# A macaron block with a selective scan: another planned order of its instructions, and the scan carries copied later

## The reference

```
x = x + 0.5 * ffn(layernorm(x))       # silu(g) * u with 1408 hidden units, ternary weights
x = x + ssm(layernorm(x))
x = x + 0.5 * ffn(layernorm(x))       # the same weights

ssm: h, gate = x @ W_in (1024 channels each)
     h = silu(causal_conv4(h))
     ts, B, C = h @ Wx, each rms-normed (128, 16 and 16 values)
     delta = softplus(ts @ Wdt + bias)
     for each channel i and n in 0..15, over time t:
         s[t] = exp(delta[t] * A[i,n]) * s[t-1] + delta[t] * B[t,n] * h[t]
     y[t] = sum over n of s[t] * C[t,n] + D * h[t];  out = (y * silu(gate)) @ Wout
```

## Time and profile before

| | us |
|---|---|
| median of three executions | 2842.37 |
| lowest, highest | 2838.3, 2843.48 |
| profiled execution, its own time | 2835.58 |
| its span, first to last instruction | 2833.8 |
| VectorE busy in the span | 2466.0 |
| TensorE busy | 2386.6 |
| GpSimd busy | 2275.5 |
| ScalarE busy | 1757.4 |
| mean granted clock of TensorE, of 1 | 0.922 |

### The profile page before, as it was taken

The page is one execution under the profiler, slowest core; times in us unless marked ns, Lnnn a source line. Parts: engine busy times, 40 slices in busy tenths (PEclk is TensorE's granted clock), DMA queues, the critical chain, the costliest instruction groups (busy, mean ns, idle before and its releaser), DMA issues. The chain is left out here.

```text
span 2833.8 us, 38163 instructions
## 1 busy us (share of the span) xinstructions
PE 2386.6 (84%) x12266; PEld 1933.5 (68%) x12266; DVE 2466.0 (87%) x3115; ACT 1757.4 (62%) x2995; POOL 2275.5 (80%) x1387
## 2 busy tenths in 40 slices
PE   6779789689577998889988999889988886599968
PEld 5657677577466776677766877677776764477756
DVE  5649997897998989899999999899989988999973
ACT  5465667767656666576657765577657666465531
POOL 2257769779976889789996999779996889889852
PEclk9889899899789999999999999999999997599979
DMA  8655645846666467955778366955778388366544
GB/s 268 225 191 167 238 160 178 297 131 230 205 214 235 127 211 265 310 172 172 248 267 314 129 216 237 322 202 166 235 266 283 121 287 289 101 206 188 183 165 141
DMA packets 293952, 606.66 MB, mean 214 GB/s; under 512 B 23024, under 2 KB 23792, under 8 KB 293744
## 3 DMA queue, kind: packets, MB, share of 16 engines
q1 hardware_dynamic: 293744, 604.13, 63.5%
HBM read 451.47 MB, written 152.57 MB: 213 GB/s over the span
## 5 line engine op out<-in xcount | busy, mean ns | idle before, releaser
L1930 POOL TENSOR_TENSOR sbuf<-dus,bring 128x1024 f32<-128x1024 f32 x512 | 1217.9, 2394 | 181.3 <-PE pt L1403 94.4
L1556 ACT ACTIVATE pa<-dls,cst 128x512 f32<-128x512 f32 x1024 | 691.8, 688 | 432.3 <-DVE sbuf L1730 415.8
L1403 PE MATMUL pt<-ident,sbuf 128*128 128x128 f32 x4096 | 645.0, 294 | 210.9 <-DVE sbuf L1730 84.1
L1403 PEld LDWEIGHTS pt<-ident,sbuf 128*128 128x128 f32 x4096 | 507.2, 150 | 367.4 <-DVE sbuf L1730 131.9
L1322 PE MATMUL pm<-xT,wring 128*128 128x512 f32 x2816 | 708.0, 399 | 16.1 <-DVE xT L1613 6.4
L1730 DVE TENSOR_TENSOR_SCAN sbuf<-pa,sbuf 128x512 f32<-128x512 f32 x512 | 610.0, 1211 | 64.6 <-ACT pa L1556 53.4
L1730 DVE TENSOR_TENSOR_SCAN sbuf<-pa,carry,sbuf 128x512 f32<-128x512 f32 x512 | 631.9, 1268 | 35.2 <-POOL sbuf L1930 23.1
L1334 PE MATMUL pm<-wring,act 128*128 128x512 f32 x2176 | 581.4, 410 | 25.1 <-DVE hd L1658 9.4
L1322 PEld LDWEIGHTS pm<-xT,wring 128*128 128x128 f32 x2816 | 516.6, 189 | 120.3 <-issue 18.4
L1741 DVE SCALAR_TENSOR_TENSOR acc<-pt,cT,acc 128x512 f32<-128x512 f32 x768 | 548.0, 739 | 51.6 <-PE pt L1403 49.9
L1334 PEld LDWEIGHTS pm<-wring,act 128*128 128x128 f32 x2176 | 401.6, 193 | 113.4 <-issue 14.4
(11 more groups left out here) (142 smaller groups left out, 2285.9 us busy)
## 6 DMA issues: line engine op xcount, KB each, us to landing
wring<-wsp SPq DMA_DIRECT2D x408, 512.0 KB, 4.5
bring<-b_d SPq DMA_DIRECT2D x256, 256.0 KB, 3.9
xn_d<-tb SPq DMA_DIRECT2D x24, 1024.0 KB, 9.1
xnb<-xn_d SPq DMA_DIRECT2D x19, 1024.0 KB, 7.3
x_d<-tb SPq DMA_DIRECT2D x16, 1024.0 KB, 6.1
u_d<-hd SPq DMA_DIRECT2D x64, 256.0 KB, 5.7
sg_d<-hd SPq DMA_DIRECT2D x64, 256.0 KB, 4.3
tb<-x_d SPq DMA_DIRECT2D x16, 1024.0 KB, 6.8
```

What stands on the lines that cost most here:

```text
L1403: ins = e.matmul(pt[u.pt[tt]][:, k * P:(k + 1) * P], sbuf[:, u.s3, k, tt * P:(tt + 1) * P], ident[:, :], is_transpose=True, start=True, st ...
L1556: e.activation(pa[k % 2][:, :], dls[:, k, :], ACT.Exp, scale=col(C_A + (4 * u.ig + k) * N + u.n)).then_inc(S.a_exp, 1)
L1930: e.tensor_tensor(sbuf[:, u.s3, h * m:(h + 1) * m, :], dus[:, h * m:(h + 1) * m, :], bring[:, u.s2:u.s2 + 1, :].broadcast_to([P, m, TC]), ...
```

## The change

The planner's costs change: MARGIN goes from 0.3 to 0.12, LATE of TensorE from 0.3 to 0.2 (the others by 0.01 or 0.02), VectorE's fixed cost from 0.05 to 0.064. TensorE's matmuls have no fixed cost any more: each is a number of columns (at least 256), and the new class Columns counts columns in stretches of 3.4133 us of the plan's time. A matmul runs at 2270 columns a microsecond in the plan where the stretch before has counted 3060 or more, else at 1200. These are constants of the plan. The emitted instructions are the same ones; their order on each engine is what the new plan gives.

The carry copy moves within ScalarE's thread s: the Book hands each step the even step before it (behind), and the copy for that one is issued after the second exponential (k == 1) of the next step. The copy of an even chunk's last step is issued in the first step of the odd chunk. A scan of an odd chunk now waits for the copy of its own ig and n, where it waited for the last copy made.

```diff
--- before.py
+++ after.py
@@ -71,10 +71,12 @@
     "sp": {},
 }
 SPARE = {("pe", "t"): 0.4, ("act", "t"): 0.0, ("pool", "t"): 0.0, ("act", "s"): 0.0, ("pool", "s"): 0.0}
-MARGIN = 0.3
+MARGIN = 0.12
 DWELL = 12.0
+
+WINDOW, BUSY, FULL, HALF_RATE = 3.4133, 3060, 2270.0, 1200.0
 ISSUE, LAND = 0.42, 2.5
-LATE = {"pe": 0.3, "act": 0.13, "dve": 0.13, "pool": 0.15}
+LATE = {"pe": 0.2, "act": 0.12, "dve": 0.14, "pool": 0.17}
 PEF = 1.12
 
 
@@ -117,6 +119,7 @@
 
     def begin(self):
         self.events, self.time, self.up, self.table = [], 0.0, None, None
+        self.columns = ()
 
     def wait_ge(self, *events):
         self.events += events
@@ -128,14 +131,14 @@
         if self.eng == "act":
             self.time += 0.09 + n / 1190.0 + more
         elif self.eng == "dve":
-            self.time += 0.05 + n / 962.0 + more
+            self.time += 0.064 + n / 962.0 + more
         else:
             self.time += 0.16 + n / 474.0 + more
         return self
 
     def matmul(self, out, a, b, is_transpose=False, **k):
         n = width(out)
-        self.time += 0.115 if is_transpose else 0.16 if n < 256 else n / 2140.0
+        self.columns += (max(256, n), 2 * n if is_transpose else n),
         return self
 
     def activation(self, out, a, f, bias=None, scale=None, **k):
@@ -181,12 +184,32 @@
         return self
 
 
+class Columns:
+
+
+    def __init__(self):
+        self.count = {}
+
+    def run(self, t, work):
+        for n, counted in work:
+            left = 1.0
+            while left > 1e-9:
+                k = int(t / WINDOW + 1e-9)
+                whole = n / (FULL if self.count.get(k - 1, 0.0) >= BUSY else HALF_RATE)
+                part = min(left, ((k + 1) * WINDOW - t) / whole)
+                self.count[k] = self.count.get(k, 0.0) + part * counted
+                left -= part
+                t += part * whole
+        return t
+
+
 class Plan:
 
 
 
     def __init__(self):
         self.reach, self.now, self.clock, self.owner = {}, {}, {}, {}
+        self.columns = Columns()
         self.table, self.switched, self.dma = None, 0.0, 0.0
 
     def order(self, threads):
@@ -232,7 +255,7 @@
                         at += 1.3
                         self.switched = at
                     self.table = s.table
-                end = at + s.time
+                end = self.columns.run(at, s.columns) if eng == "pe" else at + s.time
                 self.clock[eng] = end
                 end += LATE[eng]
             if s.up is not None:
@@ -282,6 +305,7 @@
         self.check = None
         self.stores = []
         self.scans, self.turns, self.softs = 0, 0, 0
+        self.carried, self.behind = {}, None
         self.first_stage()
 
     def up(self, sem, by=1):
@@ -969,7 +993,8 @@
                         load_u(1, 2 * h + 1)
             self.sfree["b", u.s2] = (u.prod[-1],)
             u.pa_before, u.exp, u.scan = [], [], []
-            u.carry_in = sf("carry") if second else ()
+            u.carry_in = self.carried[u.ig, u.n] if second else ()
+            u.behind = self.behind
             for k in range(4):
                 u.pa_before.append(sf(("pa", k % 2)))
                 u.exp.append(self.up(S.a_exp))
@@ -981,11 +1006,11 @@
                 self.sfree["pa", k % 2] = (u.scan[k],)
             if second:
                 self.sfree["carry_rd"] = (u.scan[3],)
-                u.carry = ()
+                u.carry, self.behind = (), None
             else:
                 u.carry_before = sf("carry_rd")
-                u.carry = (self.up(S.a_carry),)
-                self.sfree["carry"] = u.carry
+                u.carry = self.carried[u.ig, u.n] = (self.up(S.a_carry),)
+                self.behind = u
             self.add("t", u)
             u.ct = self.x_small[c].ct
             u.pt, u.pt_before, u.tr, u.acc_before, u.mul, u.sum = [], [], [], [], [], []
@@ -1556,11 +1581,12 @@
                         e.activation(pa[k % 2][:, :], dls[:, k, :], ACT.Exp,
                                      scale=col(C_A + (4 * u.ig + k) * N + u.n)).then_inc(S.a_exp, 1)
                         yield
-                    if not u.second:
-                        q.wait_ge(u.scan[3], *u.carry_before)
-                        e.activation(carry[:, u.n, 4 * u.ig:4 * u.ig + 4], sbuf[:, u.s3, :, TC - 1],
-                                     ACT.Copy).then_inc(S.a_carry, 1)
-                        yield
+                        if k == 1 and u.behind:
+                            v = u.behind
+                            q.wait_ge(v.scan[3], *v.carry_before)
+                            e.activation(carry[:, v.n, 4 * v.ig:4 * v.ig + 4], sbuf[:, v.s3, :, TC - 1],
+                                         ACT.Copy).then_inc(S.a_carry, 1)
+                            yield
             return program
 
         def act_states(units):
```

## The result

The changed kernel takes 2807.23 us (median of four runs, 2800.55 to 2812.57) against 2840.34 of the kernel before (four runs): a ratio of 0.9877, 95% interval 0.985 to 0.9905. The forecast was 2809. Its profiled execution took 2812.57 us around a span of 2810.7. That is the slowest of its four, and the profiled one of before (2835.58) was faster than all four of its own, so the two traces lie 23.1 us apart and not 33. The remaining 10 us are in no trace.

A forecast was written before the change was run, and what follows sets the result against it. The prediction took VectorE's work in a written order, plus its holes, to bound the middle. Carry -25, rates -4 and room -4 us sum to -33, taking the median 2842.4 to 2809 us; range 2775 to 2850.

The forecast's parts named there:

- The bound: Middle of the kernel: VectorE's work in a written order plus its holes, 209.5 us the most any order gives back.
- -25 for the carry: Even chunks' scans: moving the carry copy frees the next exponential, making their holes like odd chunks'; 25 us gained.
- a filled hole may only reach the next one: Even chunks' scans: reason for taking the carry's gain as 25 us, a little less than the row's 29.4.
- -4 for the rates: Middle at granted clock 0.5: planning TensorE's two rates cuts VectorE's idle time; 4 us gained, 21.2 at stake.
- -4 for the room: Hand-overs between engines: less planned room and VectorE's new fixed cost place consumers nearer to where they can run; 4 us.
- The sum: Whole kernel: carry, rates and room give -33 us, opening and tail nothing; median 2809 us.
- Its own sign of being wrong: Middle: wrong if VectorE's holes don't fall by 25 us or more; another sign was opening or tail changing by over 5.
- Slack gone: Rival at hand-overs: with 0.3 us less cover, just-in-time ones come late and holds pass on; 2872 us, chance 0.15.
- The product takes its place: Rival at the scans: they wait for GpSimd's product instead of the exponential, most gain returns; 2838 us, chance 0.18.
- The order hardly changes: Rival in the planner: same heads win, only the carry counts; 2817 us, inside the forecast's band, no separate chance.

The follow-up runs named there:

- found2: Changed kernel with other planner values (MARGIN 0.048, other LATE, SPARE and VectorE fixed cost), picked for the finished order's end in one cost table; 2786.3 us.
- carry_only: Against the kernel before: carry copy moved and the order planned anew with all the old costs; 2879.8 us, ratio 1.0131.
- margin13: Changed kernel with MARGIN 0.13 in place of 0.12 and nothing else; 2845.4 us, ratio 1.0004.
- the frozen order: Kernel before with its order kept on every engine and only the carry copies moved in ScalarE's queue; 2838.9 us, ratio 0.9983.
- costs_only: Changed kernel with the carry copy put back in its old place, all planner costs new; 2872.6 us, ratio 1.0102.

## Why the prediction was right, and where it was not

**The bound.** Right. In all fourteen kernels VectorE's busy time stays within 2457 to 2468 us, while their spans go from 2790 to 2876. All but those 11 us is its holes: 332 us in found2, 349 in the changed kernel, 368 in before, 418 in carry_only.

**Step "-25 for the carry".** Wrong as a worth of the move. The mechanism is as described: nearly all of the 0.85 us holes go, the copy never waits, and the changed kernel's product doesn't wait for it (in margin13 it does once, for 11.9 us, where the prediction put the later release at nothing). But its worth was 4.6 us in the old order, a loss of 36 planned anew with the old costs, a gain of 65 with the new ones and nothing with MARGIN 0.13. The error was to read the difference between even and odd chunks (29.4 us) as time that the end would see. A hole ahead of a scan, with queues written around it, is room that other waits fill: in the frozen order's trace 16.3 us went and 14.7 came back at the transposes. "a filled hole may only reach the next one" stood in the prediction, as a discount of 4 us; in the frozen order it was some 20 of the 25.

**Steps "-4 for the rates, -4 for the room".** Too small as parts, and no parts: from carry_only the rates give 33, the room 9, both 73. Each of these numbers is one order. The prediction took 4 for the room "since no row says which holes a new order closes"; that was the step that mattered, and no row could price it.

**The sum.** -33 forecast and -33 measured. With MARGIN 0.13 the same working would have forecast the same number and missed by 36 us. It is a right number by terms of which none is shown, and that is luck. Its own sign of being wrong, holes of the middle that fall by less than 25 us, came true (19.8).

**The rivals.** "Slack gone" is not borne out as a mechanism: found2 has a smaller MARGIN (0.048) and a smaller room at TensorE's t than the change and is faster (its ScalarE's t has 0.1 more), and margin13 has more room and is slower. "The product takes its place" is what happened in carry_only, with a price of 36 us above before and not 4 under. "The order hardly changes" was the worst reading: the order is what changes. The rival that was missing: that the planner's choice, stirred by a constant that means next to nothing, moves the time by more than any term of the sum. MARGIN's hundredth cost 38 us with the copy moved and gave 31 with it in its old place (2872.6 to 2841.5). Not every stir does that: the shifted stretches cost 8.

**What stays open.** Whether the move helps on average over many sets of costs. Of three pairs planned at equal costs one gains (2872.6 to 2807.2), one doesn't (2841.5 and 2845.4) and one loses (2843.6, the kernel before on that chip, to 2879.8). For the rates and the room nothing is known beyond their one order each. The new order with the copy put back wasn't tried. And what makes the changed kernel's order a good one isn't shown, only that it is the order.

## What to carry to other kernels

When an order comes out of a greedy planner, a measured hole is no price for the change that removes it: freeze the order to price the edit (a low price, since that order was planned without it), and move an unrelated constant by a hundredth to see how far orders scatter, before reading any gain as the edit's. Then choose the order by its own end under one fixed table of costs taken from a trace, over many sets of planning constants; here the two that were run gave 0.5% and 0.8% on top of the change without any new idea. And watch what the faster thread will run dry of: a scan that outran the stage that makes its input turned small holes into ones of over 20 us in carry_only.

## What the runs showed of the hardware

The mean granted clock goes with the order of the instructions: 0.915 to 0.927 in all executions of before, 0.902 to 0.904 in the six of costs_only. It is no measure of the time. Before had 375.5 us of its middle at 0.5 (1.2 GHz), the changed kernel 440.3, and the changed kernel is faster, with fewer VectorE holes in these stretches (44.7 us for 49.1).

The scan without a carry operand takes 1211 ns on average before, 1207 to 1210 in the eleven kernels with the copy moved, and 1211 and 1212 in the two others with it in the old place: 0.5 to 2 us over 512 scans. What shortens it isn't shown.
